# Writing out the three looped turns of the delta stage on all engines of a two-layer attention and mixture-of-experts kernel

## The reference

```python
def step(Sst, inp):
    q_t, k_t, v_t, a_t, b_t = inp
    Sst = Sst * a_t[..., None, None]
    kv = jnp.einsum('bhd,bhde->bhe', k_t, Sst)
    delta = (v_t - kv) * b_t[..., None]
    Sst = Sst + jnp.einsum('bhd,bhe->bhde', k_t, delta)
    o_t = jnp.einsum('bhd,bhde->bhe', q_t, Sst) * scale
    return (Sst, o_t)
...
gate = (h @ Wg).reshape(b, s, H, DV)
o = rms_norm(o) * o_norm_w * jax.nn.silu(gate)
return o.reshape(b, s, H * DV) @ Wo
```

## Time and profile before

| what | value |
|---|---|
| median of 3 runs | 2167.25 us (2164.94 to 2167.41) |
| span of the profiled execution | 2169.9 us |
| turn 0, 1, 2, 3 of the delta stage | 207.18, 207.29, 202.61, 210.18 us |
| TensorE busy in the span | 1755.3 us (81%) |

### The profile page before, as it was taken

One profiled execution on the slowest core, in us unless ns is written; L12 is line 12 of the kernel. 1 busy time (PEld: TensorE's weight loads), 2 busy tenths in 40 slices (PEclk: granted clock), 3 DMA queues, 4 the chain that ended last, 5 costly groups with the idle time before them and its releaser, 6 DMA issues. The chain is left out here.

```text
span 2169.9 us, 38141 instructions
## 1 busy us (share of the span) xinstructions
PE 1755.3 (81%) x12097; PEld 1251.1 (58%) x12097; DVE 1296.5 (60%) x3411; ACT 1062.4 (49%) x3153; POOL 878.0 (40%) x1091
## 2 busy tenths in 40 slices
PE   2258871998419985999968899999999999899977
PEld 1124440887419872656647677777777777555533
DVE  5557773453634537778857666556666666455556
ACT  0015330443114432878944466666666666666643
POOL 0003556455565551434434874423324251622233
PEclk9999775999559995999979999999999999999988
DMA  8310001432312225000003322121212122110001
GB/s 343 137 39 2 19 22 39 115 99 68 112 45 71 67 71 170 21 24 29 27 27 81 80 55 64 35 65 35 69 43 70 44 56 54 51 47 28 26 11 39
DMA packets 155839, 135.76 MB, mean 63 GB/s; under 512 B 88085, under 2 KB 128214, under 8 KB 153494
## 3 DMA queue, kind: packets, MB, share of 16 engines
q1 hardware_dynamic: 144278, 98.03, 16.1%
q0 software_dynamic: 9088, 18.70, 2.7%
q10 hardware_dynamic: 2304, 16.91, 1.9%
HBM read 77.03 MB, written 56.54 MB: 62 GB/s over the span
## 5 line engine op out<-in xcount | busy, mean ns | idle before, releaser
L2671 DVE TENSOR_TENSOR delta_sv<-delta_sv,delta_zp 32x256 f32<-32x256 f32 x384 | 161.2, 420 | 170.5 <-PE delta_zp L2312 164.3
L813 POOL DMA_INDIRECT y<-moe_y,moe_aim x156 | 177.4, 1137 | 159.5 <-DVE moe_y L1306 67.6
L1766 ACT ACTIVATE field_p<-field_sp,field_nm 128x128 f32<-128x128 f32 x512 | 180.3, 411 | 0.8 <-DVE field_nm L1850 0.7
L2584 POOL TENSOR_TENSOR delta_dd<-delta_ll,delta_minus 128x1024 f32<-128x1024 f32 (+1 forms) x9 | 23.7, 2636 | 377.9 <-DMA delta_ll<-lanes 377.8
L2591 POOL TENSOR_TENSOR delta_dd<-delta_dd,delta_prod 128x30 f32<-128x30 f32 (+11 forms) x270 | 154.5, 572 | 21.2
L2589 POOL TENSOR_TENSOR delta_prod<-delta_ll,delta_dd 128x30 f32<-128x30 f32 (+11 forms) x270 | 141.4, 524 | 21.2
L2312 PE MATMUL delta_zp<-delta_sv,delta_ct 128*32 128x128 f32 x1536 | 122.5, 281 | 20.3 <-DVE delta_sv L2671 12.4
L2280 PE MATMUL delta_xp<-delta_la,delta_di 128*128 128x256 f32 x512 | 121.4, 391 | 12.6 <-DMA delta_di<-inverses 6.7
L1766 ACT ACTIVATION_READ_ACCUMULATOR field_p<-field_sp,field_nm 128x1 f32 x512 | 128.4, 251 | 0.0
L2312 PEld LDWEIGHTS delta_zp<-delta_sv,delta_ct 128*32 128x32 f32 x1536 | 70.3, 110 | 85.2 <-DVE delta_sv L2671 50.8
L2280 PEld LDWEIGHTS delta_xp<-delta_la,delta_di 128*128 128x128 f32 x512 | 97.2, 194 | 37.5 <-issue 25.0
(11 more groups left out here) (552 smaller groups left out, 4638.3 us busy)
## 6 DMA issues: line engine op xcount, KB each, us to landing
delta_al<-alpha SPq DMA_DIRECT2D x33, 512.0 KB, 4.3
pairs<-c_none ACTq DMA_DIRECT2D x16, 1032.0 KB, 28.3
moe_xg<-pairs SPq DMA_DIRECT2D x78, 129.0 KB, 2.2
moe_yt<-y SPq DMA_DIRECT2D x16, 512.0 KB, 4.5
w_E<-in_E_dram SPq DMA_DIRECT2D x1, 4624.0 KB, 25.4
w_E<-in_E_dram SPq DMA_DIRECT2D x8, 578.0 KB, 3.9
lanes<-delta_la SPq DMA_DIRECT2D x128, 32.0 KB, 1.7
delta_di<-inverses SPq DMA_DIRECT2D x64, 64.0 KB, 2.4
```

What stands on the lines that cost most here:

```text
L813: nc.gpsimd.indirect_dma_start(results, bass.IndirectOffsetOnAxis(ap=aim[:, t % AR, j:j + 1], axis=0), y[:, t % YS, j, :], None).then_inc( ...
L1766: last = nc.scalar.activation(p[:, slot, h, :], s_ps[i][:, k, :], ACT.Exp, bias=nm[:, slot, h:h + 1], accum_out=zs[:, slot, h:h + 1])
L2671: nc.vector.tensor_tensor(sv[rows, two, :], sv[rows, two, :], z_ps[2 * pair // HH][rows, at, :], ALU.subtract).then_inc(s["z_kept"], 1)
```

## The change

`turns` becomes a plain Python loop over all four turns, SyncE calls it too, and GpSimd's loop becomes a Python loop. The program thus holds each of the 32 rows written out on every engine, in the same order of work, and each count, each row's place in memory and each chain count (`ch.turn`) is a constant. No tile, no matmul and no transfer is added or taken away. Line numbers behind `turns` fall by 3 in the changed file, those behind SyncE's loop by 9.

```diff
         def turns(eng, step, begin=lambda t: None):
 
 
-            with eng.Fori(0, ROW_TURNS - 1) as t:
+            for t in range(ROW_TURNS):
                 begin(t)
                 for k in range(RING):
                     step(t, k)
-            begin(ROW_TURNS - 1)
-            for k in range(RING):
-                step(ROW_TURNS - 1, k)
 
         def looped(t):
-            return not isinstance(t, int) or t < ROW_TURNS - 1
+            return t < ROW_TURNS - 1
...
-                    if isinstance(t, int) and t == 0 and k == 1:
+                    if t == 0 and k == 1:
...
-                for k in range(RING):
-                    step(0, k)
-                with sp.Fori(1, ROW_TURNS - 1) as t:
-                    for k in range(RING):
-                        step(t, k)
-                for k in range(RING):
-                    step(ROW_TURNS - 1, k)
+                turns(sp, step)
...
-                with pool.Fori(0, ROW_TURNS - 1) as t:
+                for t in range(ROW_TURNS - 1):
                     ch.turn(t, 2 * each, before)
                     for k in (GB, 2 * GB):
                         inverses(Row(t, k))
```

## The result

The changed kernel's median is 2155.55 us of 12 runs (2151.03 to 2170.64), against 2167.33 us of 12 runs (2161.24 to 2171.07) of the kernel before in the same series. I predicted 2157.5. The medians differ by 11.8 us; the ratio, which carries the interval, is 0.9952 (95%: 0.9938 to 0.9966), that is, 10.4 us less, between 7.4 and 13.4. Two later series with the same kernel gave 0.9944 (0.9931 to 0.9958) and 0.9931 (0.9915 to 0.9947).

The account below looks back on a forecast made before the run. TensorE was taken to bound the turns. Back edges and register steps removed, less collisions, bring three turns from 617.08 to 607.30 us, a gain of 9.8, so 2157.5 us, range 2152.5 to 2161.5.

Parts of the forecast that it names:

- What bounds the turns: Delta stage's eight-row turns: TensorE is the clock, so only shortening its order of work or a wait in it helps.
- The back edges, 7.83 us: Where the loop goes back, before rows 8 and 16: idles of about 3 us and lowered clock go, 7.83 us gained.
- The rival that the 3 us aren't removed: Waits at rows 8 and 16 stay or move; only register steps gain, 3.15 us, giving 2164.1 us; chance 0.06.
- Registers, 0.16 us a row: Register steps before waits on TensorE (first solve wave) and VectorE (third) go; ordinary rows fall from 25.28 to 25.12 us.
- The rival that only the back edges count: Semaphore waits replacing register steps cost the same; gain only 6.8 us, giving 2160.5 us; chance 0.10.
- Collisions in rows 8 and 16, 0.60 us each: GpSimd's first operation lengthens VectorE's L2662 there as in k = 4 rows; 25.72 us each, taking back 1.20 us.
- the rival by which rows 8 and 16 stay free: GpSimd's start shifts, so no collision there; 1.20 us kept, gain 11.0 us, giving 2156.2 us; chance 0.20.
- Row 0, 1.42 us above an ordinary row: First row of turn 0 starts slow after waiting for the first inverses; this 1.42 us stays after the change.
- Everything else stays: Outside the three turns nothing changes, so the profiled span falls from 2169.9 to 2160.1 us.
- The slower rival: Straight code waits for its own instructions at 42 TensorE fetch crossings; at 1.5 us each, 2220 us; chance 0.02.

Follow-up runs that it names:

- hinted loop: Kernel before, loops and registers kept, with each pass's top instruction naming the loop's head to be fetched; ratio to before 0.9973, turns 611.0 us.
- TensorE alone in the loop: Changed kernel with TensorE's turns looped as before, all other engines written out; ratio to before 0.9983, turns 616.4 us.
- near branch: Changed kernel plus an empty two-pass loop between turns on TensorE, ScalarE and VectorE; ratio to before 0.9933, turns 605.8 us.
- the pair of mixed kernels: Changed kernel with only TensorE looped as before (0.9983 of before), and with only VectorE and ScalarE looped (0.9973).
- the one-pass loop: Changed kernel with its three written-out turns inside a loop of one pass; ratio to before 0.9934, turns 608.4 us.

## Why the prediction was right

**What bounds the turns: right.** TensorE's order of work does. A register step of 0.08 us on it shows in the row, and a stall of VectorE shows only as far as TensorE waits for it (1.65 of 2.94 us).

**The back edges, 7.83 us: right.** The hinted loop takes out the fetch and nothing else. Rows 7 and 15 fall from 28.23 and 28.04 us to 25.12 each, 6.0 us; no row 8 or 16 has the 1.68 us of the lowered clock in the ten executions without a stall of TensorE's back edge, and row 16 has it in the other two that have such stalls, at a granted clock of 0.76 both times (before's second execution, and TensorE alone in the loop). The rival that the 3 us aren't removed is refuted, by the near branch and by the hint. The Trainium skill's rule that a taken branch out of the two-page window waits for a fetch (Runtime: NRT & Kernel Launch, Instruction fetch mechanics) agrees with 208 ns to a near target and 3312 to 3852 ns to a far one; the size of the window no run here tests. The Trainium skill's figure of about 108 ns (Advanced Engine Details and Errata, Control Flow Timing) lies between TensorE's branch not taken, 76 to 88 ns, and taken to a near target, 208 ns.

**Registers, 0.16 us a row: right.** The changed kernel's wait at TensorE's first wave in all 32 rows, against the earlier trace rows, and its third wave on VectorE in row 10, against 0.84 in the earlier trace rows:

```profile
L2293 PEldq EVENT_SEMAPHORE  x32: 51/830/1682, 1236.7 to 2023.9; - x32
...
1493.55 1.32 DVE L2662 TENSOR_TENSOR delta_sv<-delta_sv,delta_zp 32x256 f32<-32x256 f32 x3 [0.75 <-PE delta_zp L2303]
```

The two waits that the register step had carried on TensorE don't stand with the matmul in the trace, as the order of the changed program suggests, but in a semaphore wait of their own. It is the cheaper of the two all the same: the rows take 25.28 us with the steps of both sides, 25.20 with either side's, 25.12 with neither. The rival that only the back edges count fell with that; what kills it is the pair of mixed kernels, not the one-pass loop, which had lost its registers.

**Collisions in rows 8 and 16, 0.60 us each: right in mechanism, wrong in place and size, and right in sum by luck.** I expected five rows of 25.72, 3.0 us. The first execution had 2.95, but as 0.60, 0, 1.45, 0.46 and 0.44. That its three turns came to 607.32 us against 607.30 is therefore chance; the next two executions had 606.6 and 607.0. (The prediction's reading of turn 2 also slips: the 0.8 us and the 2.22 us are of row 12, as the earlier trace rows says; row 20 had 2.15 us.) The step that failed is that GpSimd's start is fixed in the row. It begins between 8.2 and 10.1 us into it, by when the lanes arrive, in the same program from one execution to the next: row 8 was free in the first execution and took 25.70 and 25.93 us in the next two. The three executions lose 2.95, 2.45 and 2.7 us, the kernels with near branches and with the one-pass loop 1.6 and 4.0. So the rival by which rows 8 and 16 stay free came half true in the first execution and in neither of the next two, while there row 12 came free.

**Row 0, 1.42 us above an ordinary row: too little.** It took 26.69 us, 1.57 more, and 26.48 and 26.60 us in the next two executions.

**Everything else stays: not shown.** I predicted a span of 2160.1; it was 2148.6. Of the 11.5 us, 7.7 lie ahead of the turns, where executions of one kernel differ by as much as 6 us. The other 3.9 lie behind row 24, and there the two kernels do part: 320.1 and 321.2 us in the two executions of before, 316.2 to 316.5 in three of the changed kernel, 315.0 to 318.7 in all others. Busy time by stretch, from row 24 to the end, before and after (the first row is of before):

```profile
1849.82:2169.91 320.09, 273.65 (x1226) 150.98 (x1222) 181.53 (x294) 172.72 (x420) 105.56 (x121) 0.94 0.12 34
```

```profile
1832.39:2148.61 316.22, 271.78 (x1226) 150.33 (x1222) 184.06 (x294) 172.63 (x420) 105.06 (x121) 0.95 0.11 35
```

The place can be told. From the start of row 24 to that of row 31 the first execution of either kernel takes 183.9 us, each row the same within 0.05 us. The 3.9 us all lie behind: 136.2 us from the start of row 31 to the end before, 132.3 after. Busy time over the 50 us that begin 200 us behind row 24's start, before and after (the first row is of before):

```profile
2049.82:2099.82 50.00, 37.92 (x125) 19.15 (x125) 26.56 (x40) 17.11 (x45) 10.78 (x10) 0.83 0.04 13
```

```profile
2032.39:2082.39 50.00, 39.48 (x133) 20.08 (x132) 28.52 (x42) 18.88 (x47) 13.68 (x13) 0.90 0.04 13
```

Before, TensorE gets through eight matmuls fewer there, at the lower clock. From row 31's start to the end the second execution of before takes 138.7 us, the next two of the changed kernel 132.6 and 132.5, and all eight others 134.7 to 135.7. The time of arrival doesn't order them: the kernel with TensorE alone in the loop starts row 24 at 1847.9 us, nearly as late as before, and takes 134.8. With this stretch, the later ratios of 0.9944 and 0.9931 (12 and 15 us) are less odd beside turns that give 10 to 12. What decides the clock there stays open.

**The slower rival: refuted.** No row shows a wait of straight code for its instructions: an ordinary row lasts the same 25.12 us in turn 0 and in turn 2. In place of the earlier trace rows, the list of waits of the changed kernel has only weight loads at this line, 0.4 us at most; and the queue that I counted 42 blocks on moved 34 in the three turns, against 40 before:

```profile
PEld delta_xp L2271 <- issue: 9.9, 24, 0.4
```

```profile
q8 instruction: 34, 0.56, 0.4%
```

## What to carry to other kernels

Look at the way back of each hardware loop whose body is long. On TensorE compare the branch's duration with that of the way out. On VectorE and ScalarE the branch's record doesn't hold the stall (55 to 74 ns and 40 to 50 ns here); look for idle time with "issue" right behind it (2.94 us on VectorE). Where one of them lasts microseconds, the price is the fetch of the loop's head, once a pass, and writing the turns out or naming the head in time both remove it; the first also removes register steps (0.08 us a row for TensorE's and as much for VectorE's here), the second keeps the program short. Before pricing such a stall, ask which engine's stall the bounding engine feels, because stalls of several engines at one place don't add. And when a kernel is as regular as this, list the rows that aren't of the ordinary length: here a single wait on GpSimd, which idled some 60 us before most of its inversions, made all but row 0 ordinary.

## What the runs showed of the hardware

- A compare-and-branch on TensorE took 76 to 88 ns not taken, 208 ns taken to a target a few instructions away, 357 and 376 ns taken to a far target that was named ahead, and 3312 to 3852 ns taken to a far one that wasn't.
- Whether GpSimd's loop pays it is not shown: its branches took 40 to 55 ns, but ScalarE's record is no longer with 2.03 us of idle behind it, and GpSimd's waits of some 63 us for its lanes would hide a fetch.
- VectorE's L2653 ends about 0.54 us behind the end of a GpSimd operation that began before it, be it 0.1 or 1.1 us before. The later GpSimd starts ahead of it, the dearer it gets (0.45 us a row at 8.2 us into the row, 1.45 at 9.2), until it starts behind and costs nothing. The same GpSimd operation, begun 0.08 us ahead of VectorE's scan L2647, made that 4.57 us in place of 2.28.
- That cliff makes the turns of one program differ by some tenths from one execution to the next (2.45 to 2.95 us of collisions) with nothing changed.
- TensorE's granted clock was 0.76 over the 7 us behind one of the two stalls of 2.7 to 3.3 us in each of the three executions that have them (row 8, 16 and 16, behind 3.05, 2.99 and 3.21 us), and 1.00 behind the other one (2.85, 3.27 and 2.73 us). The length of the stall doesn't tell the two apart.
